# A selective-scan block with a feed-forward layer: six moves in a hand-written order of instructions

## The reference

```python
def attn(x):                                  # x: 4096 x 1024
    x_, z = split(layernorm(x) @ in_proj_w)   # 2048 channels each
    xc = silu(conv4(x_))                      # causal, 4 taps
    dt_r, B, C = rmsnorm each of (xc @ x_proj_w.T)     # 64, 16, 16
    dt = softplus(dt_r @ dt_proj_w + dt_bias)
    for t: h = exp(dt * A) * h + dt * B * xc  # 2048 channels x 16 states
           ys = sum over states of h * C
    return ((ys + D * xc) * silu(z)) @ out_proj_w
x = x + attn(x)
x = x + layernorm(x) @ dequantised(W).T + bias         # 1024 x 1024
```

## Time and profile before

| | us |
|---|---|
| median of 3 runs (lowest, highest) | 4797.93 (4795.17, 4798.03) |
| the profiled execution, its own time | 4799.74 |
| its span in the profile | 4797.9 |

### The profile page before, as it was taken

How to read it: one execution, slowest core, us unless ns; L and a number is a source line. 1 busy time by engine, 2 the same in 40 slices (tenths; PEclk the granted TensorE clock), 3 DMA queues, 4 the chain that set the end, 5 groups by cost and what they waited for, 6 DMA issues and landing times.

```text
span 4797.9 us, 72703 instructions
## 1 busy us (share of the span) xinstructions
PE 4492.0 (94%) x22816; PEld 3927.0 (82%) x22816; DVE 4167.9 (87%) x5745; ACT 3576.0 (75%) x8976; POOL 4025.0 (84%) x2910
## 2 busy tenths in 40 slices
PE   7778889999999999999999999999999999998889
PEld 6567778888888888888888888888888888887678
DVE  3898889989899998989989898998989999898981
ACT  4677777877777777787877777777777777777760
POOL 0888879989898988989889898998989898898980
PEclk9789989999999999999999999999999999999999
DMA  7324243343433435343343434434343343434232
GB/s 252 126 77 152 103 148 129 125 170 136 175 118 137 164 126 180 122 174 131 117 178 125 178 134 149 145 125 169 136 176 117 135 168 126 169 121 145 90 111 93
DMA packets 160257, 678.09 MB, mean 141 GB/s; under 512 B 21120, under 2 KB 30080, under 8 KB 110720
## 3 DMA queue, kind: packets, MB, share of 16 engines
q1 hardware_dynamic: 141440, 639.88, 37.3%
q10 hardware_dynamic: 18432, 33.56, 1.9%
HBM read 618.32 MB, written 55.05 MB: 140 GB/s over the span
## 4 chain that ended last, share of the span: by engine, by line
PE 45%; POOL 25%; issue 13%; DVE 9%; ACT 5%; DMA 2%; SPq 1%; POOLq 0%; DVEq 0%; ACTq 0%
POOL dbx L489 16%; PE gx L594 13%; PE g L764 11%; PE ys L574 11%; DVE hb L1364 5%; POOL half L497 5%; PE ys L614 2%; DVE hc L1312 2%; PE ys L604 2%; PE ys L624 2%; POOL x L505 1%; DMA b_scratch<-ssmT 1%; POOL dtx L516 1%; PE hb L857 1%; ACT dt L1008 1%
## 5 line engine op out<-in xcount | busy, mean ns | idle before, releaser
L1364 DVE TENSOR_TENSOR_SCAN hb<-hb,dbx 128x512 f32<-128x512 f32 x2048 | 2499.3, 1220 | 326.7 <-ACT hb L1073 275.2
L489 POOL TENSOR_TENSOR dbx<-dtx,bb 128x1024 f32<-128x1024 f32 x1024 | 2418.3, 2362 | 62.9 <-DVE hb L1364 38.2
L1073 ACT ACTIVATE hb<-dt,a_neg 128x256 f32<-128x256 f32 x4096 | 1789.3, 468 | 66.3
L497 POOL TENSOR_TENSOR half<-hc 128x512 f32<-128x512 f32 x1024 | 1302.0, 1272 | 216.4 <-DVE hc L1312 216.3
L1312 DVE TENSOR_TENSOR hc<-hb,cb 128x512 f32<-128x512 f32 x2048 | 1378.2, 673 | 0.0
L574 PE MATMUL ys<-half,ident 128*128 128x256 f32 x4096 | 1123.7, 399 | 198.0 <-POOL half L497 197.8
L574 PEld LDWEIGHTS ys<-half,ident 128*128 128x128 f32 x4096 | 772.5, 197 | 366.8 <-POOL half L497 262.5
L614 PE MATMUL ys<-xnT,wz 128*128 128x256 f32 x4096 | 932.8, 381 | 39.6 <-DVE ybuf L1323 39.6
L764 PE MATMUL g<-ybuf,wo 128*128 128x256 f32 x3840 | 929.9, 386 | 0.6 <-issue 0.6
L594 PE MATMUL gx<-xnT,wx 128*128 128x256 f32 x3968 | 900.7, 380 | 2.3 <-issue 1.6
L614 PEld LDWEIGHTS ys<-xnT,wz 128*128 128x128 f32 x4096 | 770.3, 191 | 147.5 <-DVE ybuf L1323 47.6
(11 more groups left out here) (114 smaller groups left out, 2966.8 us busy)
## 6 DMA issues: line engine op xcount, KB each, us to landing
wz<-in_win SPq DMA_DIRECT2D x128, 1024.0 KB, 4.8
wx<-in_win SPq DMA_DIRECT2D x124, 1024.0 KB, 4.8
wo<-in_wout SPq DMA_DIRECT2D x123, 1024.0 KB, 4.9
wf<-wf_scratch SPq DMA_DIRECT2D x113, 512.0 KB, 3.4
xc_scratch<-xcn ACTq DMA_DIRECT2D x128, 256.0 KB, 2.1
xcs<-xc_scratch SPq DMA_DIRECT2D x128, 256.0 KB, 5.1
bb<-bc_scratch SPq DMA_DIRECT2D x64, 512.0 KB, 8.2
cb<-bc_scratch SPq DMA_DIRECT2D x64, 512.0 KB, 7.7
```

The lines of the kernel that those rows point to most:

```text
L489: nc.gpsimd.tensor_tensor(dbx[:, k % 2, :].rearrange("p (n t) -> p n t", n=NQ), dtx[:, S % 2, a, :].unsqueeze(1).to_broadcast([P, NQ, T]), ...
L497: nc.gpsimd.tensor_tensor(half[:, k % 4, :], hc[:, k % 2, 0:HALF], hc[:, k % 2, HALF:GW], ALU.add).then_inc(halves, 1)
L1073: ins = nc.scalar.activation(h[:, m * T:(m + 1) * T], dt[:, j % 2, a, :], ACT.Exp, scale=a_neg[:, ds((2 * j + a) * N + 2 * v + m, 1)])
L1364: nc.vector.tensor_tensor_scan(h[:], h[:], dbx[:, k % 2, w * UW:(w + 1) * UW], 0.0, ALU.mult, ALU.add).then_inc(scans, 1)
```

## The change

1. Units ahead of softplus: on ACT units 11 and 12 stand before the taps and the softplus, unit 13 right after it, then the first decays; the chunk's RMS steps and `ss_out` come one or two units earlier, and the first skip term moves behind unit 4.
2. Taps two scans on: DVE does `y_gate` and scans 11 and 12 before the six taps.
3. B and C rows first: at a chunk's end SP stores and reloads B and C before it loads wo; PE's `ss_transpose` moves ahead of `x_in_proj(1)`.
4. Bias by quarters: four additions of 2 x 256 columns in steps 0, 2, 4 and 6 in place of two of 1024 in step 0.
5. Output blocks by token rows: ybuf is the stationary operand and the weights move, 128 columns for each half of the tokens, so the block needs no copy and no transpose.
6. Second sums: for groups 1 and 5 POOL folds 512 columns further to 256, behind a semaphore of its own, and PE adds them with one matmul in place of two. PE's group 0 moves behind `out_proj(1)` in the plain steps.

```diff
@@ SP, step
                         load_pair(S + PAIRS + 2)
-                    if nx.outproj:
-                        sp.wait_ge(o_mm, after(S - PAIRS + 1))
-                        sp.dma_start(wo[:]..., wout[jn]).then_inc(wo_in, 16)
                     if last and st.inproj:
                         bc_rows(c + 1)
                         for q in range(2):
                             load_b(c + 1, q)
                             load_c(c + 1, q)
+                    if nx.outproj:
+                        sp.wait_ge(o_mm, after(S - PAIRS + 1))
+                        sp.dma_start(wo[:]..., wout[jn]).then_inc(wo_in, 16)
@@ POOL
-                nc.gpsimd.tensor_tensor(half[:, k % 4, :], hc[:, k % 2, 0:HALF], hc[:, k % 2, HALF:GW],
+                both = nc.gpsimd.tensor_tensor(half[:, k % 4, :], hc[:, k % 2, 0:HALF], hc[:, k % 2, HALF:GW],
+                                               ALU.add)
+                if k % NQ != 1:
+                    both.then_inc(halves, 1)
+                    return
+                both.then_inc(pair_sums, 1)
+                pool.wait_ge(pair_sums, after(2 * S + k // NQ + 1))
+                nc.gpsimd.tensor_tensor(half[:, k % 4, 0:T], half[:, k % 4, 0:T], half[:, k % 4, T:HALF],
                                         ALU.add).then_inc(halves, 1)
-            def add_bias(chunk, tt):
-                pool.wait_ge(l2_ready, after(2 * chunk + tt + 1))
+            def add_bias(chunk, i):
+                pool.wait_ge(l2_ready, after(2 * (chunk + 1)))
                 pool.wait_ge(consts_in, landed(8))
-                rows = x2[:, chunk % 2, tt * H:(tt + 1) * H]
-                nc.gpsimd.tensor_tensor(rows, rows, biasb[:], ALU.add).then_inc(bias_add, 1)
+                w = H // 4
+                rows = x2_rows(chunk % 2)[:, :, i * w:(i + 1) * w]
+                nc.gpsimd.tensor_tensor(rows, rows, biasb[:, i * w:(i + 1) * w].unsqueeze(1)..., ALU.add)
...
-                        if k in (5, 6) and first and st.ffn:
-                            add_bias(c - 2, k - 5)
+                        if k == 5 and j % 2 == 0 and st.ffn:
+                            add_bias(c - 2, j // 2)
@@ PE
-                for i in range(2):
+                for i in range(1 if q == 1 else 2):
...
-                            mm = nc.tensor.matmul(g1[:, 0:T], wo[:, kt, :],
-                                                  ybuf[:, (1 - st.parity) * PAIRS + kt // 2,
-                                                       (kt % 2) * T:(kt % 2 + 1) * T], ...)
+                            for tt in range(TT):
+                                mm = nc.tensor.matmul(g1[:, tt * P:(tt + 1) * P],
+                                                      ybuf[:, (1 - st.parity) * PAIRS + kt // 2,
+                                                           (kt % 2) * T + tt * P:(kt % 2) * T + (tt + 1) * P],
+                                                      wo[:, kt, :], ...)
...
+                    out_proj(1)
+                    if not (first and st.ffn or last and st.norm1):
                         group(0)
-                    out_proj(1)
                     x_in_proj(0)
                     group(1)
+                    ss_transpose()
                     x_in_proj(1)
                     group(2)
-                    ss_transpose()
                     out_proj(2)
...
                     group(4)
-                    o_transpose()
@@ ACT
                     unit(4)
+                    first_skip_term()
...
                     unit(7)
+                    rms_square()
                     unit(8)
-                    rms_square()
+                    rms_apply()
                     unit(9)
-                    rms_apply()
                     unit(10)
-                    if not (first and st.ffn or last and st.norm1):
-                        x_taps()
                     unit(11)
-                    if first and st.ffn or last and st.norm1:
-                        x_taps()
                     ss_out()
+                    unit(12)
+                    x_taps()
                     dt_softplus()
+                    unit(13)
+                    first_decays_out()
                     second_skip_term()
-                    unit(12)
-                    o_out()
-                    unit(13)
+                    unit(14)
                     norm1_start()
                     norm1_row(0)
-                    unit(14)
+                    unit(15)
                     norm1_row(1)
-                    unit(15)
@@ DVE
                     product(9)
-                    taps()
                     y_gate(S, 0)
                     scan(11)
                     product(10)
                     scan(12)
                     product(11)
+                    taps()
                     scan(13)
```

More of the change, by code:

```diff
@@ L562, in _ @@
             for chunk in (NC - 2, NC - 1):
-                for tt in range(TT):
-                    add_bias(chunk, tt)
+                for i in range(4):
+                    add_bias(chunk, i)
         @block.tensor
@@ L853, in out_block @@
                     pe.wait_ge(wo_end[j], landed(1))
-                    pe.wait_ge(o_evac, after(k - 1))
+                    pe.wait_ge(o_add, after(k - 1))
                 w = wo_home[j].rearrange("p (k b) -> p k b", k=TILES)
-                for kt in range(TILES):
-                    mm = nc.tensor.matmul(hb[j % 2][:, 0:T], w[:, kt, :],
-                                          ybuf[:, (NC - 1) % 2 * PAIRS + kt // 2, (kt % 2) * T:(kt % 2 + 1) * T],
-                                          start=(kt == 0), stop=(kt == TILES - 1))
-                mm.then_inc(o_mm, 1)
-            def out_transpose(j):
-                k = LAST - PAIRS + j
-                pe.wait_ge(o_evac, after(k + 1))
-                pe.wait_ge(o_add, after(k - 1))
-                for tt in range(TT):
-                    mm = nc.tensor.transpose(hb[2 + j % 2][:, tt * P:(tt + 1) * P],
-                                             o_rows[j % 2][:, tt * P:(tt + 1) * P], ident[:])
-                mm.then_inc(o_tr, 1)
+                for tt in range(TT):
+                    for kt in range(TILES):
+                        mm = nc.tensor.matmul(hb[j % 2][:, tt * P:(tt + 1) * P],
+                                              ybuf[:, (NC - 1) % 2 * PAIRS + kt // 2,
+                                                   (kt % 2) * T + tt * P:(kt % 2) * T + (tt + 1) * P],
+                                              w[:, kt, :], start=(kt == 0), stop=(kt == TILES - 1))
+                mm.then_inc(o_mm, 1)
             pe.wait_ge(wf_in, landed(LAST - 2 * PAIRS))
@@ L891, in _ @@
                 out_block(j)
-                if j >= 1:
-                    out_transpose(j - 1)
-            ffn_block(NC - 2, 1)
-            out_transpose(PAIRS - 1)
-            for j in range(2, PAIRS):
+            for j in range(1, PAIRS):
                 ffn_block(NC - 2, j)
@@ L1042, in _ @@
             pair_softplus(0)
+            pair_first_decays(0)
             act.wait_ge(l1_evac, after(8))
@@ L1095, in skip_term, with first_skip_term @@
                                              scale=dparam[:, ds(2 * j + a, 1)]).then_inc(done, 1)
+                    def first_skip_term():
+                        act.wait_ge(sz_act, after(S + 1))
+                        skip_term(0, dx0)
                     def x_taps():
@@ L1154, in ss_out @@
                             chunk_ss_out(c + 1)
-                    def o_out():
-                        if not st.outproj:
-                            return
-                        act.wait_ge(o_mm, after(S - PAIRS + 1))
-                        act.wait_ge(o_tr, after(S - PAIRS))
-                        nc.scalar.copy(ostage[:], g1[:, 0:T]).then_inc(o_evac, 1)
                     unit(0)
@@ L1219, in _ @@
                 norm_evac(x2nT, 4 * (NC - 2), i, (gx, ys[0])[i % 2], l2_tr, l2_evac)
-            act.wait_ge(dbxs, after(8 * LAST))
-            for j in range(PAIRS):
-                k = LAST - PAIRS + j
-                act.wait_ge(o_mm, after(k + 1))
-                act.wait_ge(o_tr, after(k - 1 if j else k))
-                nc.scalar.copy(o_rows[j % 2], hb[j % 2][:, 0:T]).then_inc(o_evac, 1)
             norm2_begin(NC - 1)
@@ L1387, in add_ffn @@
                             return
-                        dve.wait_ge(bias_add, after(2 * (c - 2 if first else c - 1)))
+                        dve.wait_ge(bias_add, after((S - 1 - 2 * PAIRS) // 2 + 1))
                         dve.wait_ge(f_mm, after(S - 2 * PAIRS))
@@ L1465, in last_ffn @@
             def last_ffn(chunk, j):
-                dve.wait_ge(bias_add, after(2 * (chunk + 1)))
+                dve.wait_ge(bias_add, after(4 * chunk + j // 2 + 1))
                 dve.wait_ge(f_mm, after(chunk * PAIRS + j + 1))
@@ L1470, in _ @@
             times_c(LAST - 1, UNITS - 1)
-            dve.wait_ge(bias_add, after(2 * (NC - 2)))
```

(1 more changed line is left out.)

38 lines of the change are left out of this document (17 added, 21 removed).

## The result

| | before | after |
|---|---|---|
| median us (4 runs each) | 4797.98 | 4718.95 |
| lowest, highest | 4795.17, 4798.12 | 4716.58, 4719.75 |
| ratio of the times (95% interval) | | 0.9836 (0.9819 to 0.9853) |

The account below looks back on a forecast made before the run. A loop of ACT's softplus, POOL's folds and PE's stretch (33.83 us a step) was the bound. Middle steps -22, first steps -22, last steps +17, chunks 0 and 1 -10, last chunk +4: -33, 4765 us; range 4710 to 4815.

Parts of the forecast that it names:

- The last step: Last step of a chunk: 39.6 us where it took 38.16, +1.4 us 12 times, +17 us in all.
- Middle laps: Softplus to softplus in the six middle steps, chunks 2 to 14: 203.0 to 201.3 us a chunk, -22 us in all.
- First step: First step of a chunk: 43.9 to 42.2 us by B and C rows first, -1.7 us 13 times, -22 us.
- Chunks 0 and 1: Chunks without feed-forward work and bias: the loop's -0.66 us counts for 15 laps, -10 us.
- Last chunk: PE has little to do, POOL is busy 94% and gets 1.92 us a step more: +4 us (0 to +13).
- The end of the program: Eight out blocks at the end gain 0.22 us and lose 0.24 each: 0.
- Blocks by token rows: Output blocks on PE: block 6.9 to 7.15 us, two transposes and ACT's copy go, nothing in sum.
- A: Rival: the gain at the chunk's start is whole, first steps save 4 us each, 4718 us; chance 0.20.
- B: Rival: POOL becomes the bound, at 1.5 us a second sum 4859 us, at 1.2 us 4812; chance 0.10.
- C: Rival: PE idles before group 7 and the clock falls in plain steps, +68 us, 4833 us; chance 0.08.
- D: Rival: nothing comes of it, POOL and the last steps eat the loop's 0.66 us, about 4795 us; chance 0.12.

Follow-up runs that it names:

- e12: The changed kernel with DVE's layernorm statistics of the first norm one step earlier (step 5 of a chunk, not step 6): 4721.79 us.
- e4: The kernel before with only the change's new orders of ACT's list and of DVE's taps and y_gate: 4753.67 us.
- e9: The changed kernel with both ACT's and DVE's lists back in the old order, the other four parts kept: 4839.19 us.
- e8: The changed kernel with the bias as two additions of 1024 columns in a chunk's first step: 4715.51 us.
- e2: The changed kernel with the second sum of group 1 alone, group 5 added in two halves by PE: 4682.52 us.
- e3: The changed kernel with wo's load back ahead of the B and C rows on SP: 4745.82 us.
- e1: The changed kernel without second sums: POOL folds every group once, PE adds two halves for every group: 4698.99 us.
- e7: The changed kernel with output blocks transposed as before, restoring ACT's copy and PE's two transposes: 4719.22 us.

## Why the prediction was right or wrong

- **The last step was the step that failed.** It was put at +1.4 us, 12 times: product 15 at 14.1 us, with a fall of the clock in half the cases. It starts at 12.81, a little before the old 13.33, PE waits 1.54 and 0.52 us, and the granted clock stays at its upper level (mean 1.00 from 2595.50 to 2632.50). 36.97 in place of 39.6 is 31 of the 46 us missed. The mechanism (DVE late, SiLU and transposes behind it) is right, as e12 shows; two terms were mis-sized. Of the 2.6 us a step, 1.3 are DVE's delay and 1.0 the fall of the clock, priced at 2 us in half the cases, which never came; the remaining 0.3 is not traced. The same reordering that frees fold 5 also frees the scans behind unit 12 here: with the orders alone (e4) product 15 is at 12.38, and with both lists back (e9) it is at 13.12 and the step takes 38.34. The prediction credited this to the plain steps and charged the last step with the wait at `y_gate` only.
- **Middle laps**: forecast 201.3 for six, measured 200.5, 10 us in all over 13 chunks. A second sum costs POOL 0.728 + 0.08 = 0.81 us, not 0.96. PE's stretch was 18.8, not 18.40. The laps range from 32.95 to 33.89, less far apart than 33.2 and 34.3; with the wide bias (e8) they still range from 32.93 to 33.86, so it was wrong that the quarters make the pattern.
- What the prediction did not see is **PE's own list**: 33.55 of 33.80 us before. "No engine bounds alone" hid it, and it decides what each part is worth: nothing for the orders in middle laps (e4), 0.43 us for the sum of group 1 (e2).
- **First step**: forecast 42.2, measured 42.3, but only in part for the reason given. The SiLU hardly moved with b0 (20.24 us after the softplus, before 20.98), as said. PE's transposes then start 2.3 us sooner, not 1.7, and PE's stretch from them to the softplus takes 1.5 us more, at a lower mean of the granted clock. Against the forecast the low spell did not get longer (6.83 us both times), but it starts 1.3 us later, and 5.0 us of it, not 1.5, lie behind the start of the transposes. The orders alone bring this step to 42.4 (e4), with the B and C rows still loaded behind wo, so that the gain is not shown to be that of the B and C rows. e3 prices these at 27 us with what they do in the steps beside. From the start of the transposes to the softplus, before and after, in the view of busy time by stretch:

```profile
2704.95:2724.99 20.04, 20.04 (x103) 17.77 (x102) 16.97 (x25) 13.32 (x36) 19.69 (x14) 0.96 0.77 291
```

```profile
2653.35:2674.87 21.52, 21.52 (x125) 20.06 (x126) 13.80 (x18) 15.88 (x41) 16.71 (x13) 0.88 0.71 267
```

- **Chunks 0 and 1**: -11.8 against -10, by other shares than the forecast's. In chunk 0 the second sums cost 8.0 us (e1), which nearly cancels what the orders give there (8.2 in e4). **Last chunk**: -0.5 against +4. The second sums do cost 9.9 us there (e1), inside the bound of 13; the orders (8.2, e9) and the early B and C rows (4.5, e3) give it back. The end of the program, from the last softplus on, was put at 0 and gave 1.7.
- **Blocks by token rows** at nothing held in the total (e7); the block of 64 instructions measures 4 x 1.79 = 7.2 us, 0.112 an instruction. By the 81 ns of the Trainium skill (TensorE: Matmul & The Clock Gate, Back-to-back issue gap) it would have taken an estimated 5.2 us; the trace does not agree.
- **The rivals.** A gave 4718 and the time is 4719, but that is luck: first steps are 42.3, not 40, and what goes beyond the forecast lies in last steps and middle laps. B fell with a sum of 0.81 us; its mechanism is real all the same, as POOL bounds the laps with bias in e2. C fell: PE idles 0.27 to 1.33 us before group 7 in the six middle laps of chunk 8, as C had it, and the granted clock stays at its upper level in all middle laps of chunks 2 to 14. D fell.

## What to carry to other kernels

In a loop over several engines write down each engine's own list beside the loop before pricing an edit: here three were within 3 us of the lap, PE within 0.25, so that an edit was worth 45 or 120 us by what else was done. An instruction added to an engine with slack is cheap or dear by its place: of two equal sums the one behind group 1 gained and the one between softplus and fold 7 cost. Reorder producer and consumer together, and price the steps that differ (first, last, without feed-forward) one by one, with the benefit of each reordering in them as well as its cost.

## What was not expected of the hardware

- A GpSimd instruction that waits for the one ahead of it idled 0.08 us where that was 512 columns wide, against 0.23 where it had 32; before the chip ran it, 0.23 was taken for both.
- From chunk 3 on, the first steps alternated between 43.1 to 43.6 and 44.1 to 44.7 us before and are 42.2 to 42.4 after. Before, the granted clock lay at its lower level for 6.83 and 10.24 us by turns at the hand-over; after, for 6.83 each time; in e7 it is 10.24 in nearly every chunk, and the chunk takes no longer. Why the longer spell came and went was not tried by itself.
- The time of a whole chunk stays within 0.3 us over six kernels whose steps differ by up to 2.2 us (the table at the end of the experiments).
